# Bias attention on one NeuronCore: the low part of the shifted row bias made two key tiles later, and the maxima units of a row block spread from another starting point

## The reference, cut to what matters

```python
scores = jnp.einsum('bnqd,bnkd->bnqk', q, k) * scale + pos   # pos = row bias + column bias
attn = jax.nn.softmax(scores, axis=-1)
out = jnp.einsum('bnqk,bnkd->bnqd', attn, v)
```

## Time and profile before

| | us |
|---|---|
| median of 3 runs (lowest, highest) | 9059.98 (9059.04, 9078.75) |
| the profiled execution's own time | 9058.93 |
| its span | 9057.3 |
| PE busy, PE weight loads busy | 8186.9 (90%), 6692.4 (74%) |
| DVE, ACT, POOL busy | 7053.5 (78%), 5710.7 (63%), 6773.9 (75%) |

### The profile page before, as it was taken

One profiled execution on the slowest core, in us unless ns is written; L12 is line 12 of the kernel. 1 busy time (PEld: TensorE's weight loads), 2 busy tenths in 40 slices (PEclk: granted clock), 3 DMA queues, 4 the chain that ended last, 5 costly groups with the idle time before them and its releaser, 6 DMA issues. The chain is left out here.

```text
span 9057.3 us, 134766 instructions
## 1 busy us (share of the span) xinstructions
PE 8186.9 (90%) x42040; PEld 6692.4 (74%) x42040; DVE 7053.5 (78%) x7887; ACT 5710.7 (63%) x14778; POOL 6773.9 (75%) x3597
## 2 busy tenths in 40 slices
PE   6999999999999675999999999967999988888798
PEld 4777777777777433888888888844777868888775
DVE  6777777777777565999999999975877737999634
ACT  4877878778788445777777777722665623544304
POOL 3877978879788444999999999930886816999605
PEclk9999999999999886999999999978999989988888
DMA  2111111111111255444444444462000010000000
GB/s 96 28 46 27 47 43 32 43 32 43 47 27 38 96 205 199 103 109 105 108 105 108 106 108 104 110 224 107 17 31 16 24 48 20 1 1 1 20 8 20
DMA packets 480217, 600.84 MB, mean 66 GB/s; under 512 B 273736, under 2 KB 294480, under 8 KB 471568
## 3 DMA queue, kind: packets, MB, share of 16 engines
q1 hardware_dynamic: 478480, 591.31, 23.0%
q10 hardware_dynamic: 1024, 1.05, 0.0%
HBM read 349.14 MB, written 157.03 MB: 56 GB/s over the span
## 5 line engine op out<-in xcount | busy, mean ns | idle before, releaser
L865 POOL TENSOR_TENSOR l_probs_low<-l_probs,l_probs_high 128x512 fp32r<-128x512 f32 x1792 | 2423.4, 1384 | 595.1 <-ACT l_probs_high L818 581.2
L1601 POOL TENSOR_TENSOR m_c_h<-m_h,m_c 128x2048 f32<-128x2048 f32 x520 | 2341.8, 4578 | 45.8 <-DVE m_h L1588 45.7
L1588 DVE TENSOR_TENSOR_SCAN m_h<-m_decay,m_ps_x 128x1024 f32<-128x1024 f32 x1040 | 2271.2, 2262 | 93.4 <-issue 61.7
L1501 PE MATMUL m_ps_y<-m_c_h,m_ident 128*128 128x256 f32 x8320 | 1977.1, 381 | 2.1 <-POOL m_c_h L1601 2.1
L923 DVE TENSOR_REDUCE l_max_by_row<-l_ps_all 128x8 f32<-128x512 f32 x2048 | 1362.4, 685 | 446.8 <-PE l_ps_all L652 408.0
L1501 PEld LDWEIGHTS m_ps_y<-m_c_h,m_ident 128*128 128x128 f32 x8320 | 1509.6, 190 | 173.6 <-POOL m_c_h L1601 4.7
L816 ACT ACTIVATE l_probs<-l_ps_all 128x512 f32<-128x512 f32 x2048 | 1232.7, 602 | 414.1 <-PE l_ps_all L694 319.0
L818 ACT ACTIVATE l_probs_high<-l_ps_all 128x512 fp32r<-128x512 f32 x2048 | 1225.2, 598 | 0.0
L2615 POOL TENSOR_TENSOR s_late<-s_late,s_products 128x1024 f32<-128x1024 f32 x352 | 858.6, 2492 | 315.4 <-ACT s_products L2597 315.3
L2155 POOL TENSOR_TENSOR l_probs_low<-l_probs,l_probs_high 128x512 fp32r<-128x512 f32 x512 | 664.9, 1305 | 564.8 <-ACT l_probs_high L2138 550.5
L1525 ACT ACTIVATE m_b_diagonals<-m_steps,m_b_rows 128x32 fp32r<-128x32 f32 x4160 | 966.8, 306 | 3.2 <-DMA m_b_rows<-b_t 2.9
(11 more groups left out here) (383 smaller groups left out, 13841.5 us busy)
## 6 DMA issues: line engine op xcount, KB each, us to landing
m_delta_u<-du_t SPq DMA_DIRECT2D x1040, 128.0 KB, 3.8
m_c<-c_windows SPq DMA_DIRECT2D x130, 512.0 KB, 4.4
l_q_and_row_bias<-l_q_parts SPq DMA_DIRECT2D x64, 512.0 KB, 5.1
du_t<-m_delta_u_high SPq DMA_DIRECT2D x128, 256.0 KB, 3.0
du_t<-m_delta_u_low SPq DMA_DIRECT2D x128, 256.0 KB, 3.0
ys<-m_y SPq DMA_DIRECT2D x256, 126.0 KB, 5.0
m_direction<-ys SPq DMA_DIRECT2D x12, 2048.0 KB, 14.0
l_xn<-xn SPq DMA_DIRECT2D x8, 2048.0 KB, 11.0
```

The source lines that it names most:

```text
L865: pool.tensor_tensor(pl[:, slot, :], pt[:, slot, :], f(ph[:, slot, :]), ALU.subtract).then_inc(low_pool, 1)
L1501: ins = pe.matmul(y_ps[:, group % 2, 0:DIRS * SPAN].rearrange("p (d t) -> p d t", d=DIRS), ident[:, :], ch[:, group % CH, :, n, :], start= ...
L1588: dve.tensor_tensor_scan(h[:, u % H, :], decay[:, pair % 2, ct, k % 2, :, :].rearrange("p n t -> p (n t)"), x_ps[:, u % X, :], 0.0, ALU.mu ...
L1601: pool.tensor_tensor(ch[:, group % CH, 2 * pair % DIRS:2 * pair % DIRS + 2, :, :].rearrange("p d n t -> p d (n t)"), h[:, 2 * pair % H:2 * ...
```

## The change

It alters two lines. The unit u of the `to_do` units is put at the rounded instead of the floored tile, and `shift_low` moves in DVE's list from position 21.9 to 23.9.

```diff
         if row_in_head + 1 < NTB:
             done, to_do = (EARLY, UNITS - EARLY) if row_in_head else (FILL, UNITS - FILL)
-            part += [(row_in_head + 1, done + u) for u in range(to_do) if u * READY // to_do == i]
+            part += [(row_in_head + 1, done + u) for u in range(to_do) if (u * READY + to_do // 2) // to_do == i]
...
                     if j + 1 < NTB:
-                        work += [(READY + 0.1, take_maxima, row + 1), (READY + 1.3, shift, row + 1), (READY + 1.9, shift_high, row + 1), (READY + 2.9, shift_low, row + 1)]
+                        work += [(READY + 0.1, take_maxima, row + 1), (READY + 1.3, shift, row + 1), (READY + 1.9, shift_high, row + 1), (READY + 4.9, shift_low, row + 1)]
```

## The result

| | before | after |
|---|---|---|
| median of 5 runs, us (lowest, highest) | 9059.98 (9058.02, 9088.26) | 8977.0 (8974.66, 9008.45) |
| ratio, 95% interval | | 0.991 (0.9893 to 0.9926) |
| the profiled execution's own time | 9058.93 | 8992.7 |
| its span | 9057.3 | 8991.1 |

The kernel became 83 us faster; forecast were 80 (8980, range 8960 to 9014). Nearly everything moved as forecast; one of the two edits, though, did not earn what I had put down to it.

The account below looks back on a forecast made before the run. PE sets the pace; only its waits cost time. Terms 86.8 + 4.9 - 11.8 + 1.2 - 1 = 80.1 us off 9058.93 give 8978.8, as a median 8980; range 8960 to 9014.

Parts of the forecast that it names:

- The wait at tile 24: Steady row blocks: PE's wait for DVE's reduce, behind back-to-back shift_low and take_low, goes; gain 1.71 us each.
- The tile with two units: Steady row blocks: the double tile moves from tile 0, where it loses 0.46 us, to tile 10; gain 0.46.
- Steady row blocks together: Row blocks 1 to 5 of a head: gain 2.17 us each, 40 in all, 86.8 us.
- Row block 0: Each head: long wait goes, but double tiles at 7 and 15 wait 0.93 us each; net gain 4.9 in all.
- Row block 6: PE's first job for the next head waits 1.68 us longer for shift_low, 7 times: loss 11.8 us.
- they just swap: Row block 6: shift_low and take_low exchange places on DVE, so shift_low ends at 420.25, not 418.57.
- In the last head: Row block 6 there has no next-head job; take_low comes earlier and its one wait goes: gain 1.2 us.
- SP: Low rows are issued later, leaving no slack before the score in row block 2 of a head: loss 1 us.
- Rivals 1: POOL goes first at shift_low's new place; 48 row blocks lose 0.5 to 0.7 us each: 9011; chance 0.22.
- 2: The wait only moves: the 1.8 us stay in another place of the row block: 9062; chance 0.09.
- rival 3: Low rows land late, PE waits at a row block's first score: 9092 with 2 us beyond; chance 0.03.
- rival 4: Row block 0's new double tiles cost nothing, more gain than forecast: 8964; chance 0.06.

Follow-up runs that it names:

- experiment 1: Kernel before the change with only shift_low moved to 23.9, max units on their old tiles: 8973.8 us, ratio 0.9891.
- experiment 2: Kernel before the change with only the max units moved, shift_low staying at 21.9: 9058.9 us, ratio 0.9995.
- experiment 8: Kernel before the change with shift_low at 23.9 in row blocks 0 to 5 alone: 8954.47 us; a second kernel, shift_low at 22.9: 9013.38 us.
- experiment 5: Changed kernel, but row block 0 keeps its old double tiles and shift_low stays at 21.9 in row block 6: 8959.12 us, ratio 0.9888.
- experiment 6: As experiment 5, but row block 0's double tiles are 0, 2, 5, 9, 11, 13 and 17: 8963.68 us, ratio 0.9897.

## Why the prediction was right, point by point

*The wait at tile 24*: right in place, mechanism and size. `shift_low` behind two reduces started at 572.84, 0.03 us before POOL's operation ended (571.13 + 1.74), went first and took 0.67. The rule of the Trainium skill (SBUF — State Buffer, "SBUF: two separate sides"), that the one that starts first gets the shared port pair for the whole instruction, would by recorded starts have had it lose: POOL is recorded 0.02 earlier. It lost in 1 of 48 row blocks. That the other one then waits for a whole operation agrees: POOL's took 1.85 where it was second (about 1.3 undisturbed), DVE's 1.82 (0.67 undisturbed).

*The tile with two units*: the step that failed. I read 0.46 us as the price of the double tile, and that tile 10 would save it. Measured, the second edit saves 0.36 alone and nothing beside the first (experiments 1, 2 and 8). The cause, a `take_low` of 1.8 at tile 29, was itself a consequence of the wait that the first edit removes. The sum came out right by luck: the first edit brings this 0.46 by itself, and the forecast put it down to the second.

*Steady row blocks together*: 2.17 forecast, 41.35 - 39.19 = 2.16 measured; 40 of them 82.6 in place of 86.8, the lost races at `divide_last` or `shift_low` (0.6 each, 5 times) making most of the difference.

*Row block 0*: net 4.9 forecast, 1.3 measured. The two waits are there as forecast (in the first head only the second); the timeline of PE at tile 7 after:

```profile
509.39 0.40 PE L652 MATMUL l_ps_all<-l_k_high_and_column,l_q_and_column_bias 128*128 128x512 f32 x1
510.53 0.50 PE L652 MATMUL l_ps_all<-l_k_high_and_column,l_q_and_column_bias 128*128 128x512 f32 x1 [0.75 <-DVE l_max_by_row L923]
```

1.14 from start to start, a loss of 0.91. Left out was the double tile 4, behind `divide_first`: 0.57 more between starts in the row block shown, 0.56 in two others, 1.12 in the last head and 0.2 or less in the other four.

*Row block 6*: -11.8 forecast; experiment 5 gives 46.5 - 45.9 = 0.6 us for each of 7 heads, 4.2. (Before, row block 6 took 45.6. The 0.3 from there to 45.9 is mostly the second unit of tile 10, a matmul of 0.23 that had stood at tile 0, ahead of the first weighing, and is no loss.) The step "they just swap" was mis-sized. `take_low` there doesn't take over `shift_low`'s 1.67, since it needs no result of `shift_high` and starts 0.08 us before that ends, in time to go ahead of POOL, as DVE's timeline after shows for the place of the earlier trace rows:

```profile
404.74 1.15 DVE L940 CAST l_row_bias_high<-l_row_bias_shifted 64x512 fp32r<-64x512 f32 x1
405.81 0.68 DVE L950 TENSOR_TENSOR l_probs_low<-l_probs,l_probs_high 128x512 fp32r<-128x512 f32 x1
406.42 1.77 DVE L944 TENSOR_TENSOR l_row_bias_low<-l_row_bias_shifted,l_row_bias_high 64x512 fp32r<-64x512 f32 x1
```

In the last head the forecast had a gain of 1.2. The wait of 1.2 for `take_low` went, but PE lost as much at four weighings further on, 0.49 of it in one wait for POOL: the row block takes 37.0 and took 36.9.

*SP*: right that nobody waits; the 1 us put down for it wasn't lost. The smallest slack, in row block 2 of a head, was 0.47 us.

That the total came out at 80 is luck too: the errors (4 in steady row blocks, 4 in row block 0 and 1 in the last head, against 8 the other way in row block 6 and 1 at SP) cancelled. Rivals 1 and 2 fell with the profile after, rival 3 was shown to begin 0.5 to 2.35 us further on, and rival 4's 8964 is near what experiment 5 reached by keeping row block 0.

## What to carry to other kernels

Where two engines wait for each other's operations in turn, as DVE and POOL do here, do not put two such operations of the in-order engine back to back ahead of a step that a third engine waits for: with two short steps between them the second was 1.77 - 0.67 = 1.1 us cheaper here. And before a second wait is priced by its own rows, ask whether it is an echo of the first; run each edit alone. A step that is moved later has a deadline: compute its slack (here 2.35 us, but 0.47 in the tightest place) before going further.

## What the runs showed of the hardware

When both engines are due within some 0.04 us, the recorded starts don't say who goes first. With `shift_low` in its new place it starts 0.02 to 0.04 us before the recorded end of POOL's operation, and POOL's next one is recorded at most 0.02 us earlier than it and never later by more than 0.003. DVE won 47 times of 48; over the six profiles with `shift_low` at 23.9 (the changed kernel twice, experiments 1, 5, 6 and 8) it won 286 of 288. A loss shows as 1.82 us in place of 0.67. In row block 6 of the changed kernel `take_low` started 0.06 to 0.17 us behind POOL's operation (405.81 behind 405.74 in the one shown) and still went first, in all eight heads, while the `take_low` of tile 29 in experiment 8, 0.07 behind POOL's 586.17, waited and took 1.77. What decides it stays open; one difference is that in row block 6 DVE's cast was still running when POOL's operation began (until 405.89).
